# Cross-attention and mixture-of-experts layer: experts with split fp32r matmuls, their weights split during attention, and the units of attention's iterations in other slots

## Chip, core and metric

The kernel runs on one core of a Trainium2 chip. The metric is device time in microseconds (us) of one execution. TensorE is called PE, VectorE DVE, ScalarE ACT, GpSimd POOL, SyncE SP. PE multiplies, DVE and ACT do the elementwise work and read PE's results from PSUM, POOL does elementwise work in SBUF and issues the indirect and the accumulating transfers, SP issues the plain ones.

## What is computed

The inputs are x of 4 batches x 512 rows x 512 columns, and a context of 4 x 512 x 512. All of it is float32.

```
x  = x + quant8(layernorm(x)) @ quant8(ctx).T          # blocks of 128, rounded to fp8 values
h  = layernorm(x)                                      # "hidden"
q, k, v = rmsnorm(h) @ q_w.T, k_w.T, v_w.T             # 16 query heads, 4 key heads, 128 columns each
q, k = rope(rmsnorm(q)), rope(rmsnorm(k))
h  = h + softmax(causal(q @ k.T / sqrt(128))) @ v @ o_w.T
t  = rmsnorm(h)                                        # 2048 tokens
w, e = top2(softmax(t @ gate_w.T))                     # 8 experts, w normalised over the two
out = x + h + sum over the two of w * (silu(t @ wg[e].T) * (t @ wu[e].T)) @ wd[e].T    # inner size 352
```

## The kernel before

**Attention, mixer().** 16 iterations, one for each batch and key head, `it = 4 * b + g`. An iteration handles 4 query heads, and every head has three places (1, 2, 3) on each engine at which other work can be put; (h, place) is called a slot. units() says what stands in a slot, and each engine then does its own part of these units in that order. The kinds: q and kv project the next iteration's queries, keys and values (project(), L578), t and u transpose them, n and m are their norms, o is the output projection of the iteration before (output(), L650). FRONT holds the next batch's first stage: cm column maxima of the context (DVE, then a reduction on POOL), cs its scales, cv, cr, cd scaling, rounding and scaling back, xb, xn, xh, xa, xv, xr, xd the same for x, xt and xp transposes and product, yn, yh, yr, ht the second norm and the transposes of h. ROUTE holds the router of the batch before: rs, rn, rt, rl. SPLIT_Q and SPLIT_O hold wq and wo: in the first iterations, raw attention weights come into a ring of three stage tiles, ACT writes the part that fp32r keeps (hi), DVE the rest (lo), and SP saves both in ws_scratch, to load them back for the later batches (load_q, load_kv, load_o).

A product of two such split operands is three fp32r matmuls, of hi with hi, hi with lo and lo with hi (SPLITS). Scores (L612) go to two PSUM banks in turn; the running minimum and the scaling are DVE's (maxima(), L1151), the exponential ACT's (L840), the normalisation POOL's and DVE's (L434, L1162). The transposes and the product with v follow two heads later (L622, L633).

SP's queue is written out by hand in the order of the iterations: raw loads, save_x1, load_ctx, save_o, save_x2, then load_q, load_kv and load_o of the iteration. add_hidden() (L402) adds h to the output in DRAM with an accumulating transfer on POOL; the last batch's is the last thing of this block.

**dispatch().** One block: DVE chooses the two experts of each token, counts them and gives every token a slot in tiles of 128 rows of one expert; 32 one-hot matrices (L1419) and as many small matmuls (L1353) turn that into indices (idg for the gathers, ids for the scatters, eoff for the offset of the expert's weights in SBUF). Meanwhile SP loads the weights of all 8 experts as they are, 2176 KB each, expert 0 at once and the others when the rows' extra columns are saved (L1325).

**experts().** 39 tiles of 128 rows. PE does, for tile i: up(i) (gate and up, L1515, 8 fp32 matmuls of 352 columns), the transposes of the next tile's x (L1506), down(i - 1) (L1532, 3 fp32 matmuls of 512), the transposes of h (L1524). The offset of the weights is loaded from SBUF into a register for each tile, and so is the number of experts that must have landed:

```
for i in range(NTILE):
    ahead = offset(i + 1) if i + 1 < NTILE else None
    pe.wait_ge(w_ready, pe.value_load(eneed[0:1, i:i + 1], min_val=1, max_val=E))
    up(i, now)
    if i + 1 < NTILE:
        transposes(i + 1)
    if i:
        down(i - 1, before)
    transposes_h(i)
```

DVE multiplies the transposed x by the norm's weights (xT, L1578), forms h from SiLU and up (hh, L1600), copies its transpose (hT, L1605) and computes the row's weight; ACT does SiLU (L1567) and the scaled copy of the result (L1560); POOL gathers rows four tiles ahead (L1484) and scatters the results with accumulation, each after the one before has landed (L1493). y has three buffers.

## Time and profile before

| | |
|---|---|
| time, median of 3 runs | 1544.74 us (1543.94 to 1544.88) |
| time of the profiled execution | 1543.88 us |
| its span, first to last instruction | 1542.1 us |
| PE busy | 1332.3 us, 86% |
| DVE, ACT, POOL busy | 786.9, 639.6, 377.8 us |
| mean granted PE clock | 0.948 of 2.4 GHz |
| attention, dispatch, experts | to 1159.5; 1167.3 to 1189.4; 1189.98 to 1542.1 us |

All times of rows are microseconds from the span's start, durations in us or ns as marked. L12 is a line of the kernel. PE matmuls are pipelined, so starts tell more than durations. An idle time in brackets stands before an instruction, with what ended it.

### The profile page before, as it was taken

The page shows a single profiled execution, that of the slowest core. Times are in us where ns is not written, and L with a number is a line of the kernel's source. Part 1 is how long each engine was busy: PE and PEld are TensorE (multiplying, and loading weights), DVE is VectorE, ACT ScalarE, POOL GpSimd, SP SyncE. Part 2 cuts the span into 40 slices and gives each one's busy share as a digit, 9 for nine tenths or more (in the row PEclk, how much of TensorE's full clock was granted, in tenths as well). Part 3 has the DMA queues.
Part 4 walks back from the last instruction along what each step waited for, and adds up shares of the span by engine and source line. Part 5 has one row for each costly group of instructions (what it writes and reads, how often), then busy time and mean ns, then how long its engine had stood idle before and what let it go on. Part 6 is the DMA issues. An engine that isn't in the chain of part 4 may idle for free. (4 is left out here: it accounts for less than half of the span.)

```text
span 1542.1 us, 20420 instructions
## 1 busy us (share of the span) xinstructions
PE 1332.3 (86%) x6416; PEld 971.2 (63%) x6416; DVE 786.9 (51%) x2389; ACT 639.6 (41%) x2114; POOL 377.8 (25%) x545
## 2 busy tenths in 40 slices
PE   2876989799799989989998999999892799999996
PEld 1564757677576767777676777777671455555653
DVE  7667756556675554577555454544525122222221
ACT  6446644455564545466454544544530111111111
POOL 0322211222222122132212223223101123332331
PEclk9897999999899999999999999999995899999998
DMA  2260324413333241223214122320218833333332
GB/s 89 90 238 21 124 81 166 157 64 129 143 83 121 70 164 56 109 83 83 109 55 161 50 91 82 104 116 4 79 55 270 315 65 69 62 62 69 66 59 40
DMA packets 44505, 156.38 MB, mean 101 GB/s; under 512 B 7089, under 2 KB 7985, under 8 KB 35185
## 3 DMA queue, kind: packets, MB, share of 16 engines
q1 hardware_dynamic: 30624, 129.89, 22.7%
q0 software_dynamic: 10848, 24.71, 9.0%
q8 instruction: 55, 0.90, 0.2%
q10 hardware_dynamic: 2928, 0.49, 0.2%
q14 instruction: 50, 0.40, 0.1%
HBM read 111.00 MB, written 44.06 MB: 101 GB/s over the span
## 5 line engine op out<-in xcount | busy, mean ns | idle before, releaser
L1151 DVE TENSOR_SCALAR_CACHE_REDUCE prob<-bank,nscale 128x128 f32<-128x128 f32 (+3 forms) x256 | 135.3, 546 | 281.7 <-PE bank L614 280.4
L434 POOL TENSOR_TENSOR prob<-prob,rtotal 128x128 f32<-128x128 f32 (+2 forms) x192 | 118.5, 623 | 431.3 <-DVE rtotal L1157 404.7
L846 ACT ACTIVATE pT<-bank 128x512 f32<-128x512 f32 (+3 forms) x256 | 104.1, 432 | 263.3 <-PE bank L622 263.0
L840 ACT ACTIVATE prob<-prob,bias 128x128 f32<-128x128 f32 (+3 forms) x256 | 144.9, 566 | 163.2 <-DVE prob L1151 161.8
L1515 PE MATMUL gu<-we,xT 128*128 x624 | 197.2, 470 | 2.3 <-DVE xT L1578 1.4
L578 PE MATMUL bank<-w_hi,hT_hi 128*128 128x512 f32 x480 | 177.1, 369 | 3.4 <-DVE rot L1116 3.4
L633 PE MATMUL bank<-pT,v 128*128 128x512 f32 (+3 forms) x512 | 176.8, 447 | 2.1 <-ACT pT L846 1.5
L578 PE MATMUL bank<-w_hi,hT_lo 128*128 128x512 f32 x480 | 165.2, 344 | 0.0
L578 PE MATMUL bank<-w_lo,hT_hi 128*128 128x512 f32 x480 | 165.1, 344 | 0.0
L411 POOL TENSOR_TENSOR r<-r,rot 128x640 f32<-128x640 f32 x60 | 96.3, 1604 | 280.1 <-DVE rot L1116 280.1
L1515 PEld LDWEIGHTS gu<-we,xT 128*128 128x128 f32 x624 | 116.6, 192 | 65.7 <-issue 5.0
L650 PE MATMUL bank<-w_hi,aT_hi 128*128 128x512 f32 x256 | 109.8, 429 | 38.4 <-DVE rot L1116 22.5
L612 PE MATMUL bank<-kT_hi,qT_hi 128*128 128x128 f32 (+3 forms) x256 | 103.5, 404 | 36.1 <-DVE prob L1151 35.8
L1578 DVE TENSOR_TENSOR xT<-xtr,wcolf 128x512 f32<-128x512 f32 x39 | 27.0, 692 | 182.3 <-PE xtr L1506 182.3
L1493 POOL DMA_INDIRECT out<-y,ids x39 | 61.9, 1586 | 229.7 <-ACT y L1560 198.9
L622 PEld LDWEIGHTS bank<-ident,prob 128*128 128x128 f32 x640 | 80.6, 145 | 47.9 <-issue 35.1
L1532 PE MATMUL dn<-we,hT 128*128 x234 | 107.0, 593 | 0.7 <-DVE hT L1605 0.7
L622 PE MATMUL bank<-ident,prob 128*128 128x128 f32 x640 | 105.1, 280 | 0.0
L578 PEld LDWEIGHTS bank<-w_hi,hT_hi 128*128 128x128 f32 x480 | 94.7, 197 | 14.5 <-DVE rot L1116 6.4
L650 PE MATMUL bank<-w_hi,aT_lo 128*128 128x512 f32 x256 | 103.5, 404 | 0.0
L650 PE MATMUL bank<-w_lo,aT_hi 128*128 128x512 f32 x256 | 103.5, 404 | 0.0
L578 PEld LDWEIGHTS bank<-w_hi,hT_lo 128*128 128x128 f32 x480 | 93.3, 194 | 11.0
(274 smaller groups left out, 2548.3 us busy)
## 6 DMA issues: line engine op xcount, KB each, us to landing
w_hi<-ws_scratch SPq DMA_DIRECT2D x24, 1024.0 KB, 5.0
w_lo<-ws_scratch SPq DMA_DIRECT2D x24, 1024.0 KB, 7.3
we<-in_wexp SPq DMA_DIRECT2D x8, 2176.0 KB, 22.4
stage<-in_wqkvo SPq DMA_DIRECT2D x40, 256.0 KB, 3.0
ws_scratch<-w_hi SPq DMA_DIRECT2D x7, 1024.0 KB, 3.9
ws_scratch<-w_lo SPq DMA_DIRECT2D x7, 1024.0 KB, 7.1
w_hi<-ws_scratch SPq DMA_DIRECT2D x12, 512.0 KB, 5.9
w_lo<-ws_scratch SPq DMA_DIRECT2D x12, 512.0 KB, 6.8
```

Of the source, the lines that this page charges most:

```text
L411: nc.gpsimd.tensor_tensor(r[:, t, :], r[:, t, :], rot[t % 2][:, :], ALU.add).then_inc(rope_added, 1)
L434: nc.gpsimd.tensor_tensor(p, p, rtotal[:, 4 * h + q:4 * h + q + 1].broadcast_to([P, KEYS[q]]), ALU.mult).then_inc(prob_ready, 1)
L578: last = nc.tensor.matmul(o, hT[a][:, k, t * P:(t + 1) * P], wkv(j, c, k) if kv else wq(j, c, k), start=(k == 0 and n == 0), stop=(k == KC ...
L612: nc.tensor.matmul(o[:, 0:KEYS[q]], qT[a][:, h, q * P:(q + 1) * P], kT[it % 2][c][:, 0:KEYS[q]], start=(n == 0), stop=False)
L622: last = nc.tensor.transpose(bank[PT + j % 2][:, (q - j) * P:(q - j + 1) * P], prob[s % (LAG + 1)][:, P_AT[q] + j * P:P_AT[q] + (j + 1) * ...
L633: nc.tensor.matmul(bank[PV][:, j * P:S], v[it % (LAG + 1)][:, j, :], pT[:, PT_AT[j]:PT_AT[j] + QS[j]], start=(j == 0), stop=(j == TT - 1)) ...
L650: last = nc.tensor.matmul(bank[t % 2][:, :], aT[a][:, (G * o + h) % RING_A, t * P:(t + 1) * P], wo(c, h), start=(h == 0 and n == 0), stop= ...
L840: nc.scalar.activation(p, p, ACT.Exp, bias=bias[:, 4 * h + q:4 * h + q + 1], scale=-1.0, accum_out=total[:, 4 * h + q:4 * h + q + 1]).then ...
L846: nc.scalar.activation(pT[:, PT_AT[j]:PT_AT[j] + QS[j]], bank[PT + j % 2][:, 0:QS[j]], ACT.Copy).then_inc(pt_copied, 1)
L1151: nc.vector.tensor_scalar(prob[(G * it + h) % (LAG + 1)][:, P_AT[q]:P_AT[q] + KEYS[q]], bank[SC + q % 2][:, 0:KEYS[q]], nscale[it % 2][:, ...
L1515: last = nc.tensor.matmul(gu[i % 2][u][:, 0:I], xT[i % 2][:, k, :], we[:, bass.ds(at + (k * GU + u * I), I)], start=(k == 0), stop=(k == K ...
L1532: last = nc.tensor.matmul(dn[i % 2][:, :], hT[i % 2][:, c, :], we[:, bass.ds(at + (KC * GU + c * D), D)], start=(c == 0), stop=(c == IC - 1))
```

## The change

1. **Experts in three fp32r matmuls each.** up() and down() use split x and h and split weights, 24 and 9 matmuls in place of 8 and 3 fp32 ones. hi_x and hi_hidden (ACT) and lo_x and lo_h's like (DVE) write the halves; the norm's weights go into the expert weights, so the multiplication of x by them is gone. On DVE, hh of a tile now comes before the x of the next.
2. **Expert weights split during attention.** 96 pieces (12 of each expert, 352 or 384 columns) go through the same stage ring in iterations 5 to 14: load, ACT's hi into one of two ehi tiles, DVE's lo in place, and two stores to wx_scratch (unit "ew").
3. **Weights in a ring of four experts.** Expert 0 is loaded in dispatch, 1 to 3 when the first four gathers have landed, 4 to 7 when the expert four before is used up. PE waits for the gate/up part and the down part apart, with one more value load per tile.
4. **Other slots** for the units of FILL, FRONT, ROUTE, SPLIT_Q and SPLIT_O, and SP's queue in the order of slots.
5. **Dispatch.** The one-hots are two operations on DVE, with a spread iota copied by ACT; the first four gathers are issued here by POOL, as soon as idg is written; the last batch's add_hidden goes to the start of experts().

```
```diff
-FILL = {(0, 1): [("u", 4)], (0, 2): [("q", 0)], (0, 3): [("kv", 0), ("q", 1)],
-        (1, 1): [("kv", 1)], (1, 2): [("q", 2)], (1, 3): [("kv", 2)],
-        (2, 1): [("q", 3)], (2, 2): [("kv", 3), ("o", 0)], (2, 3): [("n", 0), ("o", 1)],
-        (3, 1): [("m", 0), ("o", 2)], (3, 2): [("o", 3)], (3, 3): [("t", 0), ("t", 1), ("t", 2), ("t", 3)]}
...
-FRONT = ({(0, 1): [("cm", 0)], (0, 2): [("cs", 0)], (0, 3): [("cv", 0)],
-          (1, 1): [("cr", 0), ("cv", 1)], (1, 2): [("cd", 0), ("cr", 1), ("cv", 2)], (1, 3): [("cd", 1), ("cr", 2), ("cv", 3)],
-          (2, 1): [("cd", 2), ("cr", 3), ("xb", 0), ("xb", 1)], (2, 2): [("cd", 3), ("xb", 2), ("xb", 3)],
-          (3, 1): [("xn", 0)], (3, 2): [("xh", 0)], (3, 3): [("xh", 1)]},
...
+FILL = {(0, 1): (('u', 4),),
+        (0, 2): (('q', 0),),
+        (0, 3): (('kv', 0), ('q', 1)),
+        (1, 1): (('kv', 1),),
+        (1, 2): (('q', 2),),
+        (1, 3): (('kv', 2),),
+        (2, 1): (('q', 3),),
+        (2, 2): (('kv', 3),),
+        (2, 3): (('o', 0), ('n', 0), ('o', 1)),
+        (3, 1): (('m', 0), ('o', 2)),
+        (3, 2): (('o', 3),),
+        (3, 3): (('t', 0), ('t', 1), ('t', 2), ('t', 3))}
...
+FRONT = ({(0, 1): (('cm', 0), ('cs', 0)),
+          (0, 2): (('cv', 0), ('cr', 0)),
+          (0, 3): (('cv', 1), ('cd', 0)),
+          (1, 2): (('cr', 1),),
+          (1, 3): (('cv', 2),),
+          (2, 1): (('cd', 1), ('cr', 2), ('cv', 3)),
+          (2, 2): (('cd', 2), ('cr', 3)),
+          (2, 3): (('xb', 0), ('xb', 1), ('cd', 3), ('xb', 2)),
+          (3, 1): (('xb', 3), ('xn', 0)),
+          (3, 3): (('xh', 0),)},
...
-SPLIT_Q = {(3, 1): [("wq", 0), ("wq", 1)], (3, 2): [("wq", 2), ("wq", 3)], (3, 3): [("wq", 4), ("wq", 5)]}
-SPLIT_O = {(1, 1): [("wo", 0)], (1, 2): [("wo", 1)], (1, 3): [("wo", 2)], (2, 1): [("wo", 3)]}
+SPLIT_Q = {(2, 1): (('wq', 0), ('wq', 1), ('wq', 2)),
+           (3, 1): (('wq', 3), ('wq', 4), ('wq', 5))}
+SPLIT_O = {(0, 1): (('wo', 0),),
+           (1, 1): (('wo', 1), ('wo', 2), ('wo', 3))}
+
+SPLIT_E = [(0, 2), (0, 3), (1, 1), (1, 2), (1, 3), (2, 1), (2, 2), (2, 3), (3, 1), (3, 2)]
+FIRST_E = 5
+GU = 2 * I
+ECOLS = KC * GU + IC * D
+PIECES = [(k * GU + u * I, I, k) for k in range(KC) for u in range(2)] + [(KC * GU + n * IP, IP, None) for n in range(IC * D // IP)]
+NPIECE = E * len(PIECES)
+RING_E = 2
...
+    if it >= FIRST_E and slot in SPLIT_E:
+        m = (it - FIRST_E) * len(SPLIT_E) + SPLIT_E.index(slot)
+        if m < NPIECE:
+            yield "ew", m
...
+            def load_exp(m):
+                n = NRAW + m
+                if m < RING_W:
+                    sp.wait_ge(wo_lo, NIT - RING_W + m + 1)
+                else:
+                    sp.wait_ge(elo_saved[n % RING_W], 16 * ((m - RING_W) // RING_W + 1))
+                e, (at, cols, _) = m // len(PIECES), PIECES[m % len(PIECES)]
+                sp.dma_start(stage[n % RING_W][:, 0:cols], wexp[e, :, at:at + cols]).then_inc(stage_in[n % RING_W], 16)
+
+            def save_exp(m):
+                e, (at, cols, _) = m // len(PIECES), PIECES[m % len(PIECES)]
+                sp.wait_ge(exp_hi, m + 1)
+                sp.dma_start(wx_dram[e, 0, :, at:at + cols], ehi[m % RING_E][:, 0:cols].bitcast(F32)).then_inc(ehi_saved[m % RING_E], 16)
+                sp.wait_ge(exp_lo, m + 1)
+                sp.dma_start(wx_dram[e, 1, :, at:at + cols], stage[(NRAW + m) % RING_W][:, 0:cols]).then_inc(elo_saved[(NRAW + m) % RING_W], 16)
...
+                for h in range(G):
+                    for place in range(1, 4):
+                        for kind, m in units(it, h, place):
+                            if kind == "ew":
+                                save_exp(m)
+                                if m + RING_W < NPIECE:
+                                    load_exp(m + RING_W)
+                        if (h, place) == (0, 3) and g == 2 and b + 1 < B:
+                            save_x1(b + 1)
+                            if b + 2 < B:
+                                load_ctx(b + 2)
+                        if (h, place) == (2, 1) and 2 <= it <= HKV:
+                            save_o(it - 1)
+                        if (h, place) == (2, 1) and HKV <= it + 2 < NIT:
+                            load_q(it + 2)
+                        if (h, place) == (2, 2) and HKV <= it + 2 < NIT:
+                            load_kv(it + 2)
                 if it >= HKV:
                     load_o(it)
+                if it == FIRST_E - 1:
+                    for m in range(RING_W):
+                        load_exp(m)
             save_x2(B - 1)
             sp.wait_ge(x1_saved, 16 * TT * B)
+            for i in range(RING_E):
+                sp.wait_ge(ehi_saved[i], 16 * ((NPIECE - i + RING_E - 1) // RING_E))
+            for i in range(RING_W):
...
-            add_hidden(B - 1)
...
+            def hi_exp(m):
+                n, (_, cols, k) = NRAW + m, PIECES[m % len(PIECES)]
+                act.wait_ge(stage_in[n % RING_W], 16 * (n // RING_W + 1))
+                if m == 0:
+                    act.wait_ge(table_in, 16 * 3)
+                if m >= RING_E:
+                    act.wait_ge(ehi_saved[m % RING_E], 16 * (m // RING_E))
+                o, i = ehi[m % RING_E][:, 0:cols], stage[n % RING_W][:, 0:cols]
+                if k is None:
+                    nc.scalar.activation(o, i, ACT.Copy).then_inc(exp_hi, 1)
+                else:
+                    nc.scalar.activation(o, i, ACT.Copy, scale=wcolf[:, k:k + 1]).then_inc(exp_hi, 1)
...
+            def lo_exp(m):
+                n, (_, cols, k) = NRAW + m, PIECES[m % len(PIECES)]
+                dve.wait_ge(exp_hi, m + 1)
+                o, i, hi = raw[n % RING_W][:, 0:cols], stage[n % RING_W][:, 0:cols], ehi[m % RING_E][:, 0:cols].bitcast(F32)
+                if k is None:
+                    nc.vector.tensor_tensor(o, i, hi, ALU.subtract).then_inc(exp_lo, 1)
+                else:
+                    nc.vector.scalar_tensor_tensor(o, i, wcolf[:, k:k + 1], hi, ALU.mult, ALU.subtract).then_inc(exp_lo, 1)
...
-            sp.dma_start(we[:, 0:ECOLS], wexp[0]).then_inc(w_in[0], 16)
-            sp.wait_ge(extra_saved, 16)
-            for e in range(1, E):
-                sp.dma_start(we[:, e * ECOLS:(e + 1) * ECOLS], wexp[e]).then_inc(w_in[e], 16)
+            load_expert(sp, 0, False)
+            load_expert(sp, 0, True)
             sp.wait_ge(pad_saved, 16)
-            sp.wait_ge(x2_saved, 16 * B)
...
+            pool.wait_ge(extra_saved, 16)
+            pool.wait_ge(x2_saved, 16 * B)
+            pool.wait_ge(sources, 1)
+            for i in range(NG):
+                pool.indirect_dma_start(xg[i][:, :], None, row_dram, bass.IndirectOffsetOnAxis(ap=idg[:, i:i + 1], axis=0)).then_inc(x_in[i], 16)
...
-            for n in range(JT):
-                V.tensor_scalar(oh[:, n, :], iotab, lo[:, n:n + 1], None, ALU.is_equal).then_inc(onehots, 1)
+            dve.wait_ge(spread, 1)
+            for c in range(2):
+                some = slice(c * NT, (c + 1) * NT)
+                V.tensor_tensor(oh[:, :, some], iotas[:, :, some], lob[:, some].unsqueeze(1).broadcast_to([P, P, NT]), ALU.is_equal).then_inc(onehots, 1)
...
-            own.done(V.tensor_copy(idg[:, :], res[:, 1, :]))
+            V.tensor_copy(idg[:, :], res[:, 1, :]).then_inc(sources, 1)
             own.chain(V.scalar_tensor_tensor(ids[:, :], tmp[:, :], pad_row, res[:, 1, :], ALU.mult, ALU.add))
+            dve.wait_ge(sources, 1)
...
+            def landed(e, down):
+                sp.wait_ge((dn_in if down else gu_in)[e % RING_WE], 32 * (e // RING_WE + 1))
+                sp.sem_inc(dn_ready if down else gu_ready, 1)
+
+            sp.sem_inc(up_done, 1)
+            sp.sem_inc(down_done, 1)
+            for i in range(NG):
+                sp.wait_ge(x_in[i], 16)
+            for e in range(1, RING_WE):
+                load_expert(sp, e, False)
+                load_expert(sp, e, True)
+            for e in range(RING_WE):
+                landed(e, False)
+                landed(e, True)
+            for e in range(RING_WE, E):
+                tiles = sp.value_load(ecum[0:1, e - RING_WE:e - RING_WE + 1], min_val=1, max_val=NTILE + 1)
+                sp.wait_ge(up_done, tiles)
+                load_expert(sp, e, False)
+                landed(e, False)
+                sp.wait_ge(down_done, tiles)
+                load_expert(sp, e, True)
+                landed(e, True)
 
...
+            pool.dma_start(out[(B - 1) * S:B * S, :].rearrange("(t p) d -> p t d", p=P), last_acc[:, :, :], accum_op=ALU.add).then_inc(hid_added, 16)
...
-                        last = nc.tensor.matmul(gu[i % 2][u][:, 0:I], xT[i % 2][:, k, :], we[:, bass.ds(at + (k * GU + u * I), I)],
-                                                start=(k == 0), stop=(k == KC - 1))
+                        for n, (a, c) in enumerate(SPLITS):
+                            last = nc.tensor.matmul(gu[i % 2][u][:, 0:I], xT[a][i % 2][:, k, :], we[:, bass.ds(at + (c * ECOLS + k * GU + u * I), I)],
+                                                    start=(k == 0 and n == 0), stop=(k == KC - 1 and n == 2))
...
-                    last = nc.tensor.matmul(dn[i % 2][:, :], hT[i % 2][:, c, :], we[:, bass.ds(at + (KC * GU + c * D), D)],
-                                            start=(c == 0), stop=(c == IC - 1))
+                    for n, (a, b) in enumerate(SPLITS):
+                        last = nc.tensor.matmul(dn[i % 2][:, :], hT[a][i % 2][:, c, :], we[:, bass.ds(at + (b * ECOLS + KC * GU + c * D), D)],
+                                                start=(c == 0 and n == 0), stop=(c == IC - 1 and n == 2))
...
-                pe.wait_ge(w_ready, pe.value_load(eneed[0:1, i:i + 1], min_val=1, max_val=E))
+                pe.wait_ge(gu_ready, expert(i))
                 up(i, now)
                 if i + 1 < NTILE:
                     transposes(i + 1)
                 if i:
+                    pe.wait_ge(dn_ready, expert(i - 1))
...
+            def hi_x(i):
+                act.wait_ge(xtr_done, i + 1)
+                if i >= 2:
+                    act.wait_ge(up_done, i)
+                nc.scalar.activation(xT[0][i % 2][:, :, :], xtr[:, :].rearrange("p (k n) -> p k n", n=P), ACT.Copy).then_inc(xT_hi, 1)
...
+            def lo_x(i):
+                dve.wait_ge(xT_hi, i + 1)
                 if i >= 2:
-                    dve.wait_ge(up_done, i - 1)
-                nc.vector.tensor_tensor(xT[i % 2][:, :, :], xtr[:, :].rearrange("p (k n) -> p k n", n=P), wcolf[:, :].unsqueeze(2).broadcast_to([P, KC, P]),
-                                        ALU.mult).then_inc(xT_ready, 1)
+                    dve.wait_ge(up_done, i)
+                nc.vector.tensor_tensor(xT[1][i % 2][:, :, :], xtr[:, :].rearrange("p (k n) -> p k n", n=P), xT[0][i % 2][:, :, :].bitcast(F32),
...
```

## Rows read from the trace of the kernel before

**Rows 1.** Windows by stage: start:end, length; busy us (instructions) of PE, PEld, DVE, ACT, POOL; PE clock, DMA share, GB/s
```profile
645.00:924.00 279.00, 255.57 (x1355) 198.40 (x1355) 168.99 (x526) 145.78 (x517) 68.66 (x116) 0.97 0.25 87
...
1221.30:1516.90 295.60, 295.60 (x1046) 175.78 (x1046) 74.93 (x180) 44.72 (x73) 91.45 (x71) 1.00 0.36 65
```

**Rows 2.** Timeline of one expert tile in the steady state: start us, duration us, engine, line
```profile
1401.88 5.00 PE L1515 MATMUL gu<-we,xT 128*128 x16
...
1406.71 0.60 PE L1506 MATMUL xtr<-ident,xg 128*128 128x128 f32 x4
...
1406.91 0.55 ACT L1567 ACTIVATE sg<-gu,xg 128x352 f32<-128x352 f32 x1 [4.51 <-PE gu L1515]
...
1407.14 2.74 PE L1532 MATMUL dn<-we,hT 128*128 x6
...
1407.95 0.57 DVE L1600 SCALAR_TENSOR_TENSOR hh<-gu,xg,sg 128x352 f32<-128x352 f32 x1
...
1409.72 0.49 PE L1524 MATMUL htr<-ident,hh 128*128 128x128 f32 x3
...
1410.08 5.00 PE L1515 MATMUL gu<-we,xT 128*128 x16
```

**Rows 3.** What PE waited for in attention, 100 to 1140 us: total us, times, longest
```profile
PE bank L612 <- DVE prob L1151: 34.4, 16, 5.0
...
PE bank L650 <- DVE w_lo L1079: 14.3, 4, 5.0
```

**Rows 4.** Timeline, first and last of 21 consecutive fp32r matmuls of output()
```profile
1142.82 0.39 PE L650 MATMUL bank<-w_hi,aT_hi 128*128 128x512 f32 x1
...
1147.38 0.39 PE L650 MATMUL bank<-w_hi,aT_lo 128*128 128x512 f32 x1
```

**Rows 5.** Timeline of the first expert tile
```profile
1202.35 7.47 PE L1515 MATMUL gu<-we,xT 128*128 x16 [1.37 <-DVE xT L1578]
...
1210.91 0.57 DVE L1600 SCALAR_TENSOR_TENSOR hh<-gu,xg,sg 128x352 f32<-128x352 f32 x1
...
1213.05 5.00 PE L1515 MATMUL gu<-we,xT 128*128 x16 [0.97 <-issue]
```

**Rows 6.** Timeline of the last expert tile
```profile
1524.61 0.56 DVE L1605 COPY hT<-htr 128x384 f32<-128x384 f32 x1 [1.73 <-PE htr L1524]
...
1525.31 2.84 PE L1532 MATMUL dn<-we,hT 128*128 x6 [0.74 <-DVE hT L1605]
```

**Rows 7.** Timeline from attention's end to the start of dispatch
```profile
1156.33 1.30 POOL L402 DMA_DIRECT2D out<-last_acc  x1 [29.57 <-DVE last_acc L1178]
...
1159.34 0.19 DVE L1261 TENSOR_TENSOR logits<-bank,extra 128x32 f32<-128x32 f32 x1 [0.22 <-DVE extra L67]
...
1167.34 0.28 DVE L1373 TENSOR_REDUCE rtop<-logits 128x16 f32<-128x128 f32 x1 [7.81 <-PEq L157]
```

**Rows 8.** Timeline of dispatch: one-hots, indices, first gather
```profile
1181.14 5.30 DVE L1419 TENSOR_SCALAR oh<-disph,lo 128x128 bf16<-128x128 bf16 x32
...
1189.06 0.18 DVE L1435 CAST idg<-res 128x40 int32<-128x40 f32 x1
...
1190.67 1.16 POOL L1484 DMA_INDIRECT xg<-row_scratch,idg  x1 [22.66 <-POOLq L1277]
```

**Rows 9.** The seven weight loads: timeline row of their issue, landing from the view of line L1325
```profile
1181.22 4.29 SPq L1325 DMA_DIRECT2D we<-in_wexp x7
...
DMA to landing us min/median/max: 8.8/25.3/38.9
```

**Rows 10.** Indirect transfers from 1300 to 1500 us: count, median us from issue to landing
```profile
out<-y,ids POOLq DMA_INDIRECT x24, 4.8
xg<-row_scratch,idg POOLq DMA_INDIRECT x24, 4.2
```

**Rows 11.** Groups by form, 390 to 1140 us: busy us, mean ns | idle before
```profile
L1079 DVE TENSOR_TENSOR w_lo<-stage,w_hi 128x512 fp32r<-128x512 f32 x3 | 2.0, 681 | 0.0
...
L795 ACT ACTIVATE w_hi<-stage 128x512 fp32r<-128x512 f32 x3 | 1.9, 625 | 0.0
```

More of the change, by code:

```diff
@@ L94 @@
[L94 removed]
[9 rows of a table removed]
+        xg = [ctx.enter_context(nc.sbuf_tensor(f"xg{i}", [P, ROW], F32)) for i in range(NG)]
+        x_in = [ctx.enter_context(nc.semaphore(f"xg_in{i}")) for i in range(NG)]
+        dispatch(nc, dispf_d, disph_d, load_expert, logits, idg, ids, first, second, eoff, eneed, ecum, extra, xg, x_in, x2_saved, row_dram, out)
+        experts(nc, load_expert, we, gu_in, dn_in, ident, idg, ids, first, second, eoff, eneed, ecum, xg, x_in, last_acc, hid_added, row_dram, out)
```

159 lines of the change are left out of this document (100 added, 59 removed), and 9 rows, old and new, of tables (FRONT, ROUTE).

## Prediction

> **What bounds the kernel now.** I read the windows by stage first. Attention iterations that also carry the next batch's front take PE at 92% (255.57 of 279), DVE at 61% (168.99) and ACT at 52%; the expert stage from 1221.3 to 1516.9 takes PE at 100% (295.60 of 295.60) at full clock, with DVE and ACT under 26% [rows 1]. So attention is PE with some holes, and the experts are PE alone: there only PE work, or PE's order, is worth anything. Then the timeline of one expert tile. Tiles start 8.20 us apart (gate and up at 1401.88 and at 1410.08); the parts are 4.83 us for gate/up, 0.43 for the four transposes of the next tile, 2.58 for down, 0.36 for the three transposes of h [rows 2]. Then the waits of PE in attention: the holes are mostly DVE's, for scores 34.4 us and for the low half of the output weights 14.3 us in four waits [rows 3].
>
> **Experts, matmuls.** An fp32 matmul runs here as two records, so gate/up is 16 passes and down 6. The change makes each three fp32r matmuls: 24 and 9. Split matmuls of 512 columns already run in output(): 21 starts from 1142.82 to 1147.38 are 0.228 us apart [rows 4], which is 512 columns at 2.4 GHz (0.213) and 0.015 over. No 352-column one is there; by the same sum it is 0.147 + 0.015 = 0.162. Bounds: 352/512 of the row is 0.157, the whole row 0.228. I take 0.162. Gate/up is then 24 x 0.162 = 3.89, down 9 x 0.228 = 2.05, transposes 0.43 + 0.32 as now: 6.69 us of PE instead of 8.0 to 8.2.
>
> The Trainium skill (TensorE: Matmul & The Clock Gate, Back-to-back issue gap) gives streams of weight load and matmul a sustained 131 ns at 512 columns, which would make the 33 matmuls about 2 us cheaper; the row has 228 ns for the same thing, so the row decides.
>
> **Experts, the loop.** PE's sum isn't the period if the loop through the other engines is longer. The h of a tile is ready at the end of hh, 1408.52, and gate/up of the next tile starts 1.56 us later [rows 2]; in the first tile, where PE stood empty, it is 1211.48 to 1213.05, again 1.57 [rows 5]. That equality says that the sequencer sets it: three transposes, two values loaded from SBUF to registers and the first offset lie between. In the first tile PE had nothing to do in that time, so it is a latency and remains after the change. New loop: gate/up 3.9 and 0.1 for the first weights, ACT's SiLU 0.03 + 0.55 behind the records' end [rows 2] (I allow 0.2), hh 0.57, 1.57: 6.9 us. PE's 6.69 fits inside. DVE now does hh before the next tile's xT, where now hh comes behind xT and starts only at 1407.95, 0.49 us after SiLU's end [rows 2]. ACT gets two copies more per tile and DVE a second subtract: ACT some 2.4 us, DVE 2.3 us of 6.9, and the low half of x is ready at about 6.1 of 6.9. Hidden, with 0.8 us of cover.
>
> Each matmul's weights lie at a register's offset, so each needs a register operation too. The trace has no such stream that isn't bound by the array. Bound below: nothing. Above: 0.59 us, the two passes that one takes now [rows 2]. Nearest row: the last down waits for hT, 1525.17, and starts at 1525.31: 0.14 us for waking, the register operation and the dispatch [rows 6]. So I take 0.12 each. The sequencer then reaches the h wait after 32 x 0.12 + some 0.4 for transposes and waits + 0.55 for the third value load (half of the 1.57 less its rest) = 4.8 us, before h at 5.4. It is covered up to 0.14 each; beyond, the period grows by 32 times the excess.
>
> In sentences that nothing rests on: the Trainium skill (same page, Wait — 56ns, not 53.3ns?) gives 62 ns per matmul for the sequencer's microcode when hardware decode is off; 33 of these are 2.0 us, beneath the array's 6.
>
> Saving: (8.20 - 6.93) x 37 periods = 47 us. First tile: now 10.7 us from gate/up to gate/up, its 16 passes took 7.47 us against 5.00 later [rows 2, 5]; after 8.7, so -2. Last tile: gate/up and two downs less, one copy more: -1.3.
>
> **Way to the experts.** DVE ends attention at 1159.53 and starts the dispatch at 1167.34; POOL's accumulating transfer of 1 MB, issued at 1156.33, is the only work left between [rows 7]. It moves behind the dispatch, so the block ends about 0.6 after DVE: -7.2 (0 if the transfer isn't the cause). One-hots: 32 operations in 5.30 us [rows 8] become two of 2048 elements; bounds 1.3 and 2.1 each, and 16 small matmuls follow the second: -1.5 on the index chain. The ACT copy that spreads the iota lies beside some 10 us of DVE work. Gathers start right behind the indices (now 1.4 us after them, 1189.24 to 1190.67) [rows 8]. Four of them are issued over 5 us, the last lands 4.2 later (unloaded median [rows 10]): indices + 8.2. But only then does SP issue 12 loads, and only behind these does it pass on that expert 0 has landed. Seven such issues took 4.29 us, so 12 take 7.3 [rows 9]. Tile 0 starts at indices + 15.7; now it is 1189.24 to 1202.35 = 13.1 [rows 5, 8]: +2.6. Sum -6.1.
>
> **Transfers.** Experts 1 to 3 are now 2 x 2176 KB each, 13.4 MB; seven old loads (15.6 MB) landed after 38.9 us [rows 9], so about 33 us of full queues. In them lie the 1 MB accumulation (11 us alone, perhaps 20) and behind it the first scatter and gather 4, which tile 4 needs some 27 us after tile 0 starts. I charge +4 (0 to 12). Later each expert is 11 us of every 34. The scatter chain is 4.8 to landing and about 0.5 to the next issue [rows 10], 5.3 of 6.9; three y buffers and four xg buffers cover a slowed one.
>
> **Attention.** 96 pieces in iterations 5 to 14, one in 10 of 12 slots. A 512-wide copy from stage costs ACT 0.625, the subtract DVE 0.681 [rows 11]; a piece of 352 or 384 columns about 0.50 and 0.56: 48 us on ACT, 54 us on DVE, over some 600 us. PE does none. What they cost is how often DVE is late for PE. Bounds: nothing, and all 54 us. DVE stands at 61% [rows 1], and most slots have DVE waiting, so a fifth: +11. Three loads/stores a piece add 52 MB over 600 us, on queues a quarter full. SP now takes its work slot by slot; if a save waits, the next piece's load waits, three slots ahead of use. Output weights are split by slot (1,1) instead of (2,1), while output() itself moves from (2,2) to (2,3): the four waits of 14.3 us [rows 3] go, but part is given to what is late next, the q rotation and the burst of three pieces in one slot: -9. Column maxima and their scales share a slot, so DVE waits for POOL's reduction: +3 in three. The other moved units: -2, bound 15 either way. Attention: +3.
>
> **Sum.** -47 -2 -1.3 -6.1 +4 +3 = -49 us. The profiled execution took 1543.9 (span 1542.1), 0.9 below the median 1544.74. 1543.9 - 49 = about 1494.
>
> **Rivals.** (A) As summed: 1480 to 1510, chance 0.56. (B) Better: PE's own 6.69 is the period (-9), no early stall (-4), the moved slots give 10: about 1471. For it: DVE's order is freer than now. Chance 0.13. (C) Scatters and gathers are slowed by the loads in each expert and the early stall is 12: +8, and 7 x 2 more: 1516. For it: queues full for 33 us; against: the buffers. Chance 0.11. (D) The pieces sit on DVE's path to PE and cost their whole 54 instead of 11: 1537, and 1545 when the moved slots lose too. Against: DVE's 61%. Chance 0.08. (E) The other side: the sequencer can't feed the 33 register-offset matmuls. At 0.19 us each it reaches the h wait at 7.0 and the period is 8.6: 37 x 1.65 = +61, 1555. From 0.178 each there is no gain in the loop. For it: no row shows two of them in a row closer than 0.59; against: the 0.14 of the last tile [rows 6]. Chance 0.12.
>
> Range 1468 to 1532: it takes in A, B and C (0.80) and the lower part of D; A alone 1480 to 1510. This kernel's runs differ by 0.06%, and about 0.2% is what can be told from no change. Slower: E and a third of D, 0.15. Same 0.02, faster 0.83.
>
> **What would show it.** Right: expert tiles 6.8 to 7.1 apart, PE idle some 0.2 us ahead of each gate/up, starts 0.16 apart within it; no gap of 7 us after attention; tile 0 behind SP's twelfth issue; no wait for w_lo in output(). Wrong: gate/up starts over 0.18 apart (E), PE waits for DVE grown by tens of us between 435 and 1080 us (D), or transposes waiting for gathers beyond tile 4 (C).

## The result and the profile after

The kernel after takes 1467.07 us (median of 4 runs, 1458.80 to 1469.38), the one before beside it 1544.34 (4 runs): ratio 0.949, 95% interval 0.947 to 0.951, 77 us less. The forecast was 1494, and the time lies 1 us under its low end. The profiled execution took 1465.88 us, its span is 1464.1.

The two traces, stage by stage, in us (a period is the time from one tile's gate/up to the next tile's):

| stage | forecast | measured | from |
|---|---|---|---|
| attention, to the last logits | +3 | -43.9 | 1159.53 to 1115.62 |
| gap ahead of dispatch | -7.2 | -7.3 | 7.81 to 0.55 |
| dispatch to gate/up of tile 0 | +1.1 | +11.4 | 35.0 to 46.4 |
| first tile | -2 | -1.4 | 10.7 to 9.3 |
| 37 periods | -47 +4 | -35.4 | 303.7 to 268.3 |
| last tile to the end | -1.3 | -1.4 | 25.3 to 23.9 |
| sum | -49 | -78.0 | |

PE's waits in attention of the kernel after, 100 to 1100 us (total, times, longest), beside [rows 3]:

```profile
PE bank L693 <- DVE kT_lo L1286: 25.9, 10, 5.3
PE bank L669 <- DVE rot L1229: 14.9, 10, 5.8
PE bank L703 <- DVE prob L1264: 14.3, 15, 6.2
PE bank L693 <- DVE hT_lo L1166: 9.6, 3, 4.2
PE bank L724 <- ACT pT L950: 9.1, 10, 3.0
```

Scores (now L703) wait 14.3 us for DVE where they waited 34.4, and output() (now L741) waits for no w_lo. And two rows of the view that [rows 3] comes from were not weighed in the forecast. Here is the head of that view of the kernel before, down to the second of them:

```profile
PE bank L612 <- DVE prob L1151: 34.4, 16, 5.0
PE bank L602 <- DVE kT_lo L1173: 23.6, 10, 7.1
PE bank L650 <- DVE rot L1116: 22.5, 24, 2.2
```

The third line is output(): in 24 small waits of 0.6 to 2.2 us, two in most iterations, it stood for the rotation of q and kv (code: output tile 0 waits for `q_rotated`, tile 1 for `kv_rotated`). That is 22.5 us, more than the four large waits for w_lo.

The windows of the same attention stretch as in [rows 1], of the expert stage, and of iterations 1 and 8 of the kernel after:

```profile
645.00:924.00 279.00, 263.77 (x1414) 206.63 (x1413) 190.76 (x577) 162.23 (x550) 76.59 (x130) 0.98 0.56 184
1221.30:1430.00 208.70, 201.72 (x1158) 181.05 (x1157) 60.25 (x145) 61.24 (x115) 76.71 (x60) 1.00 0.57 139
...
155.50:225.20 69.70, 66.96 (x342) 50.03 (x341) 53.86 (x149) 45.77 (x152) 16.43 (x28) 0.99 0.36 127
602.80:673.30 70.50, 57.68 (x302) 45.42 (x300) 50.68 (x148) 40.84 (x144) 18.83 (x30) 0.92 0.51 165
```

PE is denser in attention than before (95% against 92%), with DVE at 68% against 61%. In the expert stage PE is no longer busy all the time: 97%.

One steady expert tile after, beside [rows 2] (timeline; x2 are two matmuls):

```profile
1402.69 0.33 PE L1657 MATMUL gu<-we,xT_lo 128*128 x1
1402.85 0.60 PE L1647 MATMUL xtr<-ident,xg 128*128 128x128 f32 x4
1403.21 0.71 PE L1675 MATMUL dn<-we,hT_hi 128*128 x2
...
1405.39 0.49 PE L1666 MATMUL htr<-ident,hh 128*128 128x128 f32 x3
1405.78 0.58 PE L1657 MATMUL gu<-we,xT_hi 128*128 x2
1406.20 0.32 PE L1657 MATMUL gu<-we,xT_lo 128*128 x1
1406.37 0.48 PE L1657 MATMUL gu<-we,xT_hi 128*128 x2
1406.68 0.32 PE L1657 MATMUL gu<-we,xT_lo 128*128 x1
...
1410.51 0.59 DVE L1762 SCALAR_TENSOR_TENSOR hh<-gu,xg,sg 128x352 f32<-128x352 f32 x1 [2.89 <-ACT sg L1728]
...
1412.26 0.49 PE L1666 MATMUL htr<-ident,hh 128*128 128x128 f32 x3
```

Most steady periods are 6.87 to 6.90 us (forecast 6.93). The gate/up pitch, the time between two starts, is 0.160 (three steps from 1406.20 to 1406.68; forecast 0.162), down is 1403.21 to 1405.39 = 2.18. The sequencer feeds all 33 matmuls at this pace, so rival E did not happen. The transposes of h start 1.16 us after h is ready (1411.10 to 1412.26), right behind down's last matmul (1412.02), so PE did not stand waiting for h.

The start of the experts, SP and PE of the kernel after, beside [rows 5, 7, 9]:

```profile
1116.17 0.29 DVE L1491 TENSOR_REDUCE rtop<-logits 128x16 f32<-128x128 f32 x1 [0.55 <-PEq L215]
```
```profile
1147.35 0.80 SPq L91 DMA_DIRECT2D we<-wx_scratch  x2
...
1151.70 0.95 SPq L91 DMA_DIRECT2D we<-wx_scratch  x2
1152.69 9.67 SPq L89 DMA_DIRECT2D we<-wx_scratch  x2
```
```profile
1131.38 4.99 PE L1471 MATMUL rps<-rhs,oh 128*128 128x80 bf16 x32 [7.43 <-DVE oh L1539]
1147.13 1.08 PE L1647 MATMUL xtr<-ident,xg 128*128 128x128 f32 x4 [10.76 <-PEq L1390]
1162.56 0.95 PE L1657 MATMUL gu<-we,xT_hi 128*128 x2 [14.35 <-SPq L1599]
```

The gap ahead of dispatch is 0.55 us. But the twelve loads took SP 15.0 us, not 7.3: the last pair alone took 9.67. And the block of the experts started 9.2 us behind the indices (1137.95), behind POOL's gathers: the last was issued at 1142.87 and landed 3.8 us later, PE's next instruction stands at 1147.13.

### The profile page after: what moved, and what is told of

Read it like the earlier page. It is cut to its first block and busy times, and to the rows that moved or that the text cites. A ratio compares the mean times of both kernels' runs of the same rounds, so it can differ in the third digit from the quotient of the medians.

```text
span 1464.1 us, 22579 instructions
## 1 busy us (share of the span) xinstructions
PE 1268.7 (87%) x6845; PEld 1022.3 (70%) x6845; DVE 838.2 (57%) x2459; ACT 719.6 (49%) x2289; POOL 383.0 (26%) x545
## 5 line engine op out<-in xcount | busy, mean ns | idle before, releaser
L1264 DVE TENSOR_SCALAR_CACHE_REDUCE prob<-bank,nscale 128x128 f32<-128x128 f32 (+3 forms) x256 | 135.0, 545 | 166.7 <-PE bank L705 166.3
L669 PE MATMUL bank<-w_hi,hT_hi 128*128 128x512 f32 x480 | 175.1, 365 | 15.0 <-DVE rot L1229 14.9
L724 PE MATMUL bank<-pT,v 128*128 128x512 f32 (+3 forms) x512 | 175.0, 444 | 9.7 <-ACT pT L950 9.1
L950 ACT ACTIVATE pT<-bank 128x512 f32<-128x512 f32 (+3 forms) x256 | 103.8, 433 | 140.6 <-PE bank L713 140.0
L1657 PE MATMUL gu<-we,xT_hi 128*128 x624 | 155.8, 332 | 17.0 <-SPq L1599 14.3
L669 PE MATMUL bank<-w_hi,hT_lo 128*128 128x512 f32 x480 | 163.7, 341 | 0.0
L669 PE MATMUL bank<-w_lo,hT_hi 128*128 128x512 f32 x480 | 163.6, 341 | 0.0
L504 POOL TENSOR_TENSOR r<-r,rot 128x640 f32<-128x640 f32 x60 | 99.9, 1666 | 189.8 <-DVE rot L1229 189.8
L1657 PEld LDWEIGHTS gu<-we,xT_hi 128*128 128x128 f32 x624 | 109.0, 190 | 23.4 <-issue 21.4
L703 PE MATMUL bank<-kT_hi,qT_hi 128*128 128x128 f32 (+3 forms) x256 | 103.6, 405 | 15.7 <-DVE prob L1264 15.7
L669 PEld LDWEIGHTS bank<-w_hi,hT_hi 128*128 128x128 f32 x480 | 93.1, 194 | 26.7 <-DVE rot L1229 18.8
L741 PE MATMUL bank<-w_hi,aT_hi 128*128 128x512 f32 x256 | 104.6, 409 | 2.7 <-issue 1.6
L1657 PE MATMUL gu<-we,xT_lo 128*128 x312 | 101.6, 326 | 0.0
L741 PE MATMUL bank<-w_hi,aT_lo 128*128 128x512 f32 x256 | 100.3, 392 | 0.0
L724 PEld LDWEIGHTS bank<-pT,v 128*128 128x128 f32 x512 | 85.5, 192 | 21.1 <-ACT pT L950 9.1
L741 PE MATMUL bank<-w_lo,aT_hi 128*128 128x512 f32 x256 | 100.1, 391 | 0.0
L669 PEld LDWEIGHTS bank<-w_hi,hT_lo 128*128 128x128 f32 x480 | 92.0, 192 | 10.8
```

What stands on the lines that cost most here:

```text
L504: nc.gpsimd.tensor_tensor(r[:, t, :], r[:, t, :], rot[t % 2][:, :], ALU.add).then_inc(rope_added, 1)
L669: last = nc.tensor.matmul(o, hT[a][:, k, t * P:(t + 1) * P], wkv(j, c, k) if kv else wq(j, c, k), start=(k == 0 and n == 0), stop=(k == KC ...
L703: nc.tensor.matmul(o[:, 0:KEYS[q]], qT[a][:, h, q * P:(q + 1) * P], kT[it % 2][c][:, 0:KEYS[q]], start=(n == 0), stop=False)
L724: nc.tensor.matmul(bank[PV][:, j * P:S], v[it % (LAG + 1)][:, j, :], pT[:, PT_AT[j]:PT_AT[j] + QS[j]], start=(j == 0), stop=(j == TT - 1)) ...
L741: last = nc.tensor.matmul(bank[t % 2][:, :], aT[a][:, (G * o + h) % RING_A, t * P:(t + 1) * P], wo(c, h), start=(h == 0 and n == 0), stop= ...
L950: nc.scalar.activation(pT[:, PT_AT[j]:PT_AT[j] + QS[j]], bank[PT + j % 2][:, 0:QS[j]], ACT.Copy).then_inc(pt_copied, 1)
```

## Experiments

Sixteen kernels ran, each timed beside the kernel before (1543.7 to 1545.1 us). Differences are between medians; "after" is 1467.1. The label of each kernel (e1 to e9, x1 to x9, z1) stands beside its result. Its own four times lie 1458.8 to 1469.4, so a difference of under some 5 us says little by itself. The traces scatter too: four kernels with the same attention code (after, x1, x2, x3) end attention at 1113.3 to 1117.8, and the 37 periods, of the same experts' code in six kernels (after, e3, e9, x5, x6, x7), take 267.5 to 273.7 us.

### Which slots shorten attention

The kernel before with all new tables (copied from the change) and nothing else:

```diff
-FILL = ..., FRONT = ..., ROUTE = ..., SPLIT_Q = ..., SPLIT_O = ...      (old)
+FILL = ..., FRONT = ..., ROUTE = ..., SPLIT_Q = ..., SPLIT_O = ...      (new)
```

> The kernel before with all five new slot tables (FILL, FRONT, ROUTE, SPLIT_Q, SPLIT_O), its own order of SyncE's transfers, its own dispatch and experts; no expert pieces. Theory 1 (the slots alone shorten attention): attention loses the whole 44 us that it lost in the kernel after, and up to 11 more since no pieces are issued: 1490 to 1501. Theory 2 (SyncE's new order, by slot, is what shortens it: the stores and loads that the weight splits wait for go out at other times): within 10 us of before, 1534 to 1545, and the w_lo waits on PE stay.

Measured (e1): 1465.28 us, ratio 0.948 (0.946 to 0.950). The tables alone are worth 80 us, as much as the whole change. SP's new order isn't needed for it. In the trace attention ends at 1081.32 instead of 1159.53. Its parts, one table at a time on the kernel before:

```diff
-SPLIT_Q = {(3, 1): [("wq", 0), ("wq", 1)], (3, 2): ..., (3, 3): ...}
-SPLIT_O = {(1, 1): [("wo", 0)], (1, 2): [("wo", 1)], (1, 3): [("wo", 2)], (2, 1): [("wo", 3)]}
+SPLIT_Q = {(2, 1): (('wq', 0), ('wq', 1), ('wq', 2)), (3, 1): (('wq', 3), ('wq', 4), ('wq', 5))}
+SPLIT_O = {(0, 1): (('wo', 0),), (1, 1): (('wo', 1), ('wo', 2), ('wo', 3))}
```

> The kernel before with only the new SPLIT_Q and SPLIT_O (query and output weight splits in earlier and fewer slots). If the late splits were the whole loss (31.7 of the net 44 us came off iterations 1, 2 and 4, where they are), 1510 to 1515, and no w_lo wait of 3 to 5 us is left on PE. If the other moved units (normalisation, quantisation, router) are what counts: over 1534. If only SyncE's order counts: 1544.

Measured (e2): 1529.57, 15.4 less, ratio 0.990 (0.988 to 0.992). No w_lo wait is left (14.3 us before), but the waits of output() for the rotation grow from 22.5 to 27.2 us. So the late splits are less than half of what iterations 1, 2 and 4 lost in the kernel after (31.7 us).

```diff
-FRONT = ({(0, 1): [("cm", 0)], (0, 2): [("cs", 0)], (0, 3): [("cv", 0)], ...
+FRONT = ({(0, 1): (('cm', 0), ('cs', 0)), (0, 2): (('cv', 0), ('cr', 0)), ...
```

> The kernel before with only the new FRONT table (the next batch's normalisation, quantisation, projection and hidden units). All five tables together took 80 us off, the two split tables alone 15. If the front units are most of the rest: 1480 to 1500. If router and output moves are: over 1530.

Measured (e6): 1535.73, 9.4 less, ratio 0.994 (0.992 to 0.996).

```diff
-ROUTE = {(0, 1): [("rs", 0), ("rs", 1)], (0, 2): [("rs", 2), ("rs", 3)], (0, 3): [("rn", 0)], ...
+ROUTE = {(0, 1): (('rs', 0), ('rs', 1)), (1, 1): (('rs', 2),), (1, 2): (('rs', 3), ('rn', 0), ('rt', 0)), ...
```

> The kernel before with only the new ROUTE table (the router of the batch before in other slots). If the router's moves are a large part of the remaining 65 us: under 1525. If not: 1538 to 1545.

Measured (e7): 1536.84, 8.3 less, ratio 0.995 (0.993 to 0.997). Neither is the rest. The last table moves a single unit:

```diff
-        (2, 1): [("q", 3)], (2, 2): [("kv", 3), ("o", 0)], (2, 3): [("n", 0), ("o", 1)],
+        (2, 1): (('q', 3),), (2, 2): (('kv', 3),), (2, 3): (('o', 0), ('n', 0), ('o', 1)),
```

> The kernel before with only the new FILL table, in which one unit moves: the first output tile (o, 0) from place (2,2) to place (2,3), ahead of n. The splits alone gave 15.4, the front units 9.4, the router 8.3, all five tables 79.7 us. If this one move is most of the remainder (in the iterations 13 to 15, where nothing else differs, an iteration is 54.9 instead of 57.3 us with all tables): 2.4 x 15 = 36 off, 1505 to 1512. If the rest is only what the tables give together: over 1535.

Measured (e5): 1502.71, 41.0 less, ratio 0.973 (0.971 to 0.974). Half of all that the tables give is one output tile standing one place later. The four parts add to 74.1 us, all five tables together gave 79.7, although two of the parts (e2 and this one) end the same w_lo waits. PE's waits of this kernel, 100 to 1060 us:

```profile
PE bank L620 <- DVE prob L1159: 34.3, 17, 5.1
PE bank L610 <- DVE kT_lo L1181: 23.1, 10, 6.6
PE bank L530 <- DVE hT_lo L1070: 4.3, 3, 1.4
```

The 22.5 us for the rotation and the 14.3 us for w_lo are both gone, the others stand as they were. How the rotation holds output() is seen in the last full iteration of the kernel before:

```profile
1065.38 0.87 PE L633 MATMUL bank<-pT,v 128*128 128x256 f32 x4
1066.87 0.51 PE L650 MATMUL bank<-w_hi,aT_hi 128*128 128x512 f32 x1 [0.61 <-DVE rot L1116]
```
```profile
1065.59 0.75 DVE L1151 TENSOR_SCALAR_CACHE_REDUCE prob<-bank,nscale 128x512 f32<-128x512 f32 x1 [5.79 <-PE bank L614]
1066.26 0.08 DVE L1151 DVE_READ_ACCUMULATOR prob<-bank,nscale 128x1 f32 x1
1066.26 0.28 DVE L1114 TENSOR_TENSOR r<-bank,tab_k_c 128x128 f32<-128x128 f32 x1
1066.46 0.21 DVE L1115 TENSOR_TENSOR rot<-bank,tab_k_s 128x64 f32<-128x64 f32 x1
1066.60 0.21 DVE L1116 TENSOR_TENSOR rot<-bank,tab_k_s 128x64 f32<-128x64 f32 x1
```

DVE had been idle 5.79 us, and the kv tile was projected (the last matmul of it at 1058.42). But DVE takes its list in order, and the maxima of the next scores stand first, which PE multiplies after output tile 0 (tile 0 starts at 1059.98, the scores at 1064.54). So PE comes to tile 1 before DVE's rotation is done. With tile 0 behind these scores, its twelve matmuls (2.7 us at [rows 4]'s pitch) cover the rotation. The clock goes with it. Iteration 1 before and in this kernel, windows as in [rows 1]:

```profile
154.60:236.00 81.40, 71.28 (x334) 53.00 (x334) 54.29 (x149) 44.61 (x150) 16.81 (x28) 0.92 0.27 98
```
```profile
154.80:229.80 75.00, 67.01 (x335) 49.70 (x334) 53.80 (x149) 44.75 (x151) 16.36 (x28) 0.98 0.29 106
```

The same work takes PE 4.3 us less of busy time, at a mean granted clock of 0.98 instead of 0.92 of 2.4 GHz. The stretches at 1.2 GHz are fewer. One of them followed the 3.44 us for which PE stood still for w_lo, up to 196.29 (windows, kernel before, then this one):

```profile
196.90:200.50 3.60, 3.60 (x10) 2.79 (x9) 0.00 (x0) 0.00 (x0) 0.31 (x1) 0.53 0.88 344
```
```profile
190.00:210.00 20.00, 18.45 (x86) 13.26 (x85) 12.73 (x38) 11.21 (x39) 5.04 (x13) 1.00 0.33 131
```

How much of the 41 us is the clock over all iterations, no run separates. The Trainium skill (TensorE: Matmul & The Clock Gate, What's actually happening) says that the clock follows how busy the array is, and the rows of iteration 1 agree: less waiting, more clock.

### What the pieces cost

The kernel after with the old tables:

```diff
-FILL = ..., FRONT = ..., ROUTE = ..., SPLIT_Q = ..., SPLIT_O = ...      (new)
+FILL = ..., FRONT = ..., ROUTE = ..., SPLIT_Q = ..., SPLIT_O = ...      (old)
```

> The kernel after with all five old slot tables; pieces, SyncE's order, dispatch and experts stay as after. Theory 1 (slots): the 44 us come back and the pieces cost up to 11 more, 1508 to 1525. Theory 2 (SyncE's order): 1465 to 1477.

Measured (e3): 1525.45, 58 above after, ratio 0.989 (0.986 to 0.991). Its attention ends at 1173.95, 14.4 us behind the kernel before: on the old tables the pieces, with SyncE's new order, cost 14, close to the 11 of the forecast. On the new tables they cost much more:

```diff
     if it >= FIRST_E and slot in SPLIT_E:
-        if m < NPIECE:
+        if False:
...
-                    sp.dma_start(we[:, at:at + KC * GU].bitcast(F32), wx_dram[e, a, :, 0:KC * GU])...
+                    sp.dma_start(we[:, at:at + KC * GU].bitcast(F32), wexp[e, :, 0:KC * GU])...
```

> The kernel after without the work on the experts' weights in attention: no loads, no 160-odd splits on ScalarE and VectorE, no stores; both halves of the experts' weights are loaded raw instead (the split and the scale of the weights are left out, the transfers to the experts keep their sizes). If the pieces are hidden: 1463 to 1467. If they cost about a fifth of their own time, as the forecast had it (11 us): 1456. If they cost all of it (54 us): 1413.

Measured (e4): 1430.31, 36.8 below after, ratio 0.925 (0.923 to 0.927); attention ends at 1079.85 instead of 1115.62. The five largest lines of PE's waits in attention show where it goes: 49.9 us without the pieces (kT_lo 19.2, rot 10.0, prob 8.8, pT 7.1, hT_lo 4.8), 73.8 with them in the kernel after. On the old tables the five largest rise only from 100.5 to 107.2 us (90 to 1100 us of the kernel before and of e3). Then one half at a time:

```diff
             def lo_exp(m):
-                dve.wait_ge(exp_hi, m + 1)
-                ...subtract...then_inc(exp_lo, 1)
+                pass
...
-                sp.wait_ge(exp_lo, m + 1)
```

> The kernel after without VectorE's half of the 96 pieces: the raw piece is stored as the low half (the subtraction is left out), ScalarE's half and all transfers stay. The pieces cost 36 us in all. If VectorE is what they load (56 us of busy time and 18 us of waits for the high half there): 1435 to 1442. If ScalarE's half or the transfers are: 1455 to 1467.

Measured (x5): 1447.86, 19.2 below after, ratio 0.938 (0.935 to 0.941).

```diff
+                    sp.wait_ge(ehi_saved[(m - RING_W) % RING_E], 16 * ((m - RING_W) // RING_E + 1))
...
             def hi_exp(m):
-                ...copy to ehi...
+                pass
...
-                sp.wait_ge(exp_hi, m + 1)
-                sp.dma_start(wx_dram[e, 0, :, at:at + cols], ehi[m % RING_E]...)
+                sp.wait_ge(stage_in[n % RING_W], 16 * (n // RING_W + 1))
+                sp.dma_start(wx_dram[e, 0, :, at:at + cols], stage[n % RING_W]...)
```

> The kernel after with the pieces' transfers alone: each raw piece is loaded and stored twice, ScalarE's and VectorE's halves of the split are left out. Without pieces the kernel took 1430, without VectorE's half 1448, with all of it 1467. If the transfers cost nothing in attention and the rest of 18 us is ScalarE's: 1430 to 1434. If the transfers cost it: 1444 to 1449.

Measured (x9): 1435.46 (1429.01 to 1438.77), ratio 0.929 (0.927 to 0.931). So of the pieces' 37 us VectorE's half is 19, ScalarE's 12, the transfers 5, taken away in this order; another order could share them out otherwise. In the profiles attention ends at 1096.86, 1082.08 and 1079.85, which gives 19, 15 and 2; what the times put on the transfers beyond that lies in the experts' periods and is no more than these scatter.

And the one moved tile inside the kernel after:

```diff
-        (2, 2): (('kv', 3),), (2, 3): (('o', 0), ('n', 0), ('o', 1)),
+        (2, 2): [("kv", 3), ("o", 0)], (2, 3): [("n", 0), ("o", 1)],
```

> The kernel after with the old FILL table alone, so that the first output tile stands in place (2,2) again. In the kernel before this one move gave 41 us: 22.5 us of waits of the output tiles for the rotation and 14.3 us for the low half of the output weights. Here the output weights are split by (1,1) in either case, so the 14.3 us should not come back: 1490 to 1496. If all of it comes back: 1508.

Measured (e9): 1498.85, 31.8 above after, ratio 0.971 (0.969 to 0.973). The w_lo wait doesn't come back, the wait for the rotation does, and is longer than the 22.5 us that the expectation took; from none to:

```profile
PE bank L733 <- DVE rot L1221: 30.8, 28, 2.2
```

### Waits that the change brought

Maxima and scales of the context in one slot. DVE and PE of the kernel after, iteration 8:

```profile
606.20 2.28 DVE L1115 TENSOR_REDUCE camax<-cb 128x16 f32<-128x2048 f32 x1
614.96 0.17 DVE L1124 TENSOR_SCALAR camax<-camaxall 128x16 f32<-128x16 f32 x1 [6.49 <-POOL camaxall L490]
```
```profile
PE bank L669 <- DVE rot L1229: 5.8, 1, 5.8
```

```diff
-FRONT = ({(0, 1): (('cm', 0), ('cs', 0)), (0, 2): (('cv', 0), ('cr', 0)),
+FRONT = ({(0, 1): (('cm', 0),), (0, 2): (('cs', 0), ('cv', 0), ('cr', 0)),
```

> The kernel after with one unit moved: the context scales (cs) one slot later than the context maxima (cm), in place (0,2), so that VectorE need not stand still for GpSimd's reduction over the partitions (6.5 us in iteration 8, three times in the kernel). If that wait is on the path: 8 to 15 us off, 1452 to 1460. If other work of VectorE's would only be late for ScalarE's next unit: 1465 to 1468.

Measured (x6): 1464.17, 2.9 less, ratio 0.948 (0.945 to 0.951), which the runs can't tell from after. The move did not end DVE's wait, it halved it, and PE's for the rotation stayed (6.1 us), so this kernel does not price the whole wait:

```profile
614.70 0.17 DVE L1124 TENSOR_SCALAR camax<-camaxall 128x16 f32<-128x16 f32 x1 [3.32 <-POOL camaxall L490]
```

```diff
-          (0, 2): (('cv', 0), ('cr', 0)), (0, 3): (('cv', 1), ('cd', 0)), (1, 2): (('cr', 1),),
+          (0, 3): (('cs', 0), ('cv', 0)), (1, 1): (('cr', 0), ('cv', 1)), (1, 2): (('cd', 0), ('cr', 1)),
```

> The kernel after with the first context units in the places that they have in the kernel before or near them: maxima in (0,1), scales and first product in (0,3), first rounding in (1,1). With the scales one place later alone 2.9 us came off, and PE still waits 6.1 us in iteration 8 for the rotation behind scales and rounding on VectorE. If that wait goes with them in the three iterations that have it: 8 to 18 us off, 1450 to 1459. If the units then fill other places that are as full: 1462 to 1468.

Measured (x7): 1463.52 (1457.20 to 1467.42), ratio 0.947 (0.944 to 0.950). Attention ends 7.5 us earlier (1108.12), more than the scatter of the four kernels with after's attention, and again in z1 below (1109.03). PE's waits for the rotation fall from 14.9 to 3.8 us, those of the scores rise from 14.3 to 20.4. The end of the span is only 2.0 earlier, since the 37 periods took 273.7 us here. So the gain in attention is shown, a gain in time is not.

The way to the experts:

```diff
+            landed(0, False)
+            landed(0, True)
             for i in range(NG):
                 sp.wait_ge(x_in[i], 16)
...
-            for e in range(RING_WE):
+            for e in range(1, RING_WE):
```

> The kernel after with one edit: SyncE passes on that expert 0 has landed before it issues the loads of the experts 1 to 3; the gathers stay in the dispatch. With the gathers moved too, the way to the first gate/up product became 30.1 us instead of 46.9, and 9.1 us came off in all. If the 15 us of issuing was the whole wait: the way is 32 to 34 us. If the block's start, which waits for the gathers, is the next limit: 36 to 38 us. In time 1458 to 1463, since the tiles 4 and 5 give part back in both.

Measured (x1): 1458.08 (1454.52 to 1467.17), ratio 0.946 (0.942 to 0.950). The way from the last logits to gate/up is 34.2 us instead of 46.9. With the gathers moved to the experts' block as well (four lines from one POOL queue to the next):

> The kernel after with two edits between dispatch and experts: SyncE passes on that expert 0 has landed before it issues the loads of the experts 1 to 3, and the first four gathers are issued in the experts' block instead of the dispatch's. The way from the last logits to the first gate/up product is 46.4 us in the kernel after, of which 14.3 us is PE waiting for SyncE and 9.2 us lies between the list of rows and the block's start. If both waits are on the path, it shortens to 28 to 34 us: 1449 to 1456. If what replaces them is the gathers' own time and the loads only come later: 1462 to 1468.

Measured (x2): 1457.97 (1448.17 to 1461.90), ratio 0.944 (0.939 to 0.948); the way is 30.1 us. PE's row now says DMA where it said SP:

```profile
1140.57 1.11 PE L1648 MATMUL xtr<-ident,xg 128*128 128x128 f32 x4 [6.55 <-DMA xg<-row_scratch,idg]
```

The way is 17 us shorter, the time 9: the 37 periods from tile 1 on take 276.8 us instead of 268.3 (274.9 in x1), above the scatter of the others. Tiles 4 and 5 follow 12.7 and 11.3 us behind their predecessors. Gather 4 stands on POOL behind the first scatter, which waits for tile 0's result, and it landed 10.9 us after its issue, beside the loads of the weights, where 4.2 is [rows 10]'s median; PE waited 3.2 us for it:

```profile
1141.96 1.48 POOL L1629 DMA_DIRECT2D out<-last_acc  x1
1160.87 1.65 POOL L1635 DMA_INDIRECT out<-y,ids  x1 [17.43 <-ACT y L1709]
1162.82 1.02 POOL L1625 DMA_INDIRECT xg<-row_scratch,idg  x1 [0.30 <-issue]
1172.20 1.59 POOL L1635 DMA_INDIRECT out<-y,ids  x1 [8.36 <-DVE hh L1763]
```

In x1, where the accumulation of h was issued 3.6 us later, it is the accumulation that holds the first scatter and gather 4 behind it:

```profile
1167.67 1.65 POOL L1636 DMA_INDIRECT out<-y,ids  x1 [20.62 <-DMA out<-last_acc]
```

More buffers, the kernel after with

```diff
-NG = 4
+NG = 6
```

> The kernel after with six gather buffers instead of four. In the tiles 4 to 21, while weights load, the periods lose 13.7 us against the steady 6.88. If late gathers are the cause: 8 to 13 us off, 1454 to 1459. If the loads and stores themselves are too slow or the two more gathers ahead of the start cost their own time: 1465 to 1470.

Measured (x3): 1461.54, 5.5 less, ratio 0.946 (0.944 to 0.948); the periods take 262.3 us instead of 268.3, less than in any kernel with four buffers, and PE waits 2.0 us for gathers instead of 6.1. The way to the experts is 2.4 us longer (49.3), with two more gathers to issue. Of the stall of the tiles 4 to 21 (13.7 us over 6.88 a period) nearly half was late gathers. All together (x2, x3, x7):

> The kernel after with the edits that helped alone, together: landing passed on first and gathers in the experts' block (9.1), six gather buffers (5.5), context units later (3.5). If they add up: 1449. If the buffers also take the 8.5 us that the tiles 4 and 5 gave back after the earlier start: 1441 to 1447. If the loads of the weights are what holds those tiles up: 1450 to 1456.

Measured (z1): 1445.57 us (1439.41 to 1446.46), ratio 0.935 (0.933 to 0.938): 21.5 less than after, where the single gains add to 18; the runs can't tell these two sums apart. It beats both kernels.

## Why the forecast missed

**The step that failed** is the attention term, "Attention: +3". It was a sum of terms whose mechanisms were named and whose sizes were off. "The four waits of 14.3 us go [...]: -9", "+3 in three" for the maxima and "The other moved units: -2, bound 15 either way" stand for all the moved slots, together -8: measured 80 us less (e1). "A fifth: +11" stands for the pieces: 37 us measured (e4). Net -43.9 in the traces instead of +3, more than the whole miss of 27 us; the way to the experts and the stalls took 18 back.

Why the slots were mis-sized: of [rows 3]'s view only two lines were read, and the 24 small waits for the rotation, 22.5 us, were priced at nothing. The move of output() was seen as cover for w_lo alone; the q rotation even appears as what would be late next. And no wait was counted above its length, though in iteration 1 PE's clock rose when they went. One unit's move gave 41 us; the waits that it ended are 22.5 + 14.3 = 36.8 (e5).

Why the pieces were mis-sized: their price depends on the tables. On the old ones they cost 14 (forecast 11), on the new ones 36 in attention. A likely reason is that the new tables close the holes that hid them, but that is argued: e3 and e4 show the two prices, no run shows why they differ. The forecast took its price from the busy share of DVE in the kernel before, not from the kernel that the other parts of the change leave. Rival D had a good part of this right (37 of its 54 us) and its time, 1537, far off, because it too left the slots' 80 us out; its 1545 even let them lose.

**What held.** Steady period 6.87 to 6.90 (forecast 6.93), pitch 0.160 (0.162), gap ahead of dispatch -7.3 (-7.2), last tile -1.4 (-1.3). The period needs a word: the loop that the forecast took as its bound was there, gate/up started 1.55 us or a little more after h was ready (forecast 1.57). But PE's own parts were 3.94 + 0.35 + 2.18 + 0.36 = 6.83 us, not 6.69, as down took 2.18 instead of 2.05 (and the transposes of h 0.36, as in [rows 2], where the sum has 0.32). So loop and sum lay 0.04 us apart instead of 0.24, and these tiles can't show which of the two bounds them: rival B's "PE's own 6.69 is the period" failed in its size, not in its mechanism.

**What else was off.** The way to the experts: SP's twelve issues were priced by the seven of [rows 9], at 0.61 us each, 7.3 in all; they took 15.0. That tile 0 waits behind them was foreseen, and x1 shows it: the way is 12.7 us shorter without it. "Indices + 8.2" for the gathers became 9.2 to the block's start. The one-hots fell from 5.30 to 2.4 us, but the 32 small matmuls behind them then set the indices (4.99 us), so the chain kept its 21.8 us. The stall "+4 (0 to 12)" was 13.7, spread over the tiles 4 to 21. That is rival C's mechanism, with its sign (transposes that wait for gathers beyond tile 4, 6.1 us in five waits), at about half of what C charged in all (12 and 14 us); x3 shows that late gathers are 6 of it. The rest is open.

## What to carry to other kernels

Price every line of the waits view, the many short waits before the few long ones: 24 waits of 0.6 to 2.2 us were worth more here (31.8 us, e9) than four of 3.6 on average (15.4 us, e2). Where engines take hand-written lists in order, look at what stands in front of the releasing instruction in its own list, not at how busy its engine is. And price added work in the kernel as the other parts of the same change leave it, not in the one before: here the same pieces cost 14 us or 36.
